# A second attention with three banks for each kind of scores, small reciprocals carried by DMA, and its copies moved one unit earlier

## What is computed

```python
h = N_HEAD                                      # 8
qk = jnp.einsum('bhdq,bhdl->bhql', qh, kh) * scale
sm = jax.nn.softmax(qk, axis=-1)
ret = jnp.einsum('bhql,bhdl->bhdq', sm, vh)     # 8 rows per head, 256 x 256 scores
return gamma * ret.reshape(B, Dv, Lq)
```

## Time and profile before

| what | value |
|---|---|
| time, median of 3 runs | 710.08 us (710.06 to 710.14) |
| the profiled execution's own time | 703.4 us |
| its span, first to last instruction | 701.7 us |
| mean granted clock | 0.946 of 2.4 GHz |
| PE busy over the span | 621.0 us (88%) |
| DVE, ACT, POOL busy | 497.5, 416.4, 309.3 us |
| second attention | about 258.6 to 508 us |
| of it, steps with both a tile `v` and a tile `t` | 15, about 14.0 us each |

### The profile page before, as it was taken

How to read it: one execution, slowest core, us unless ns; L and a number is a source line. 1 busy time by engine, 2 the same in 40 slices (tenths; PEclk the granted TensorE clock), 3 DMA queues, 4 the chain that set the end, 5 groups by cost and what they waited for, 6 DMA issues and landing times. The chain is left out here.

```text
span 701.7 us, 16803 instructions
## 1 busy us (share of the span) xinstructions
PE 621.0 (88%) x5077; PEld 463.5 (66%) x5077; DVE 497.5 (71%) x885; ACT 416.4 (59%) x829; POOL 309.3 (44%) x430
## 2 busy tenths in 40 slices
PE   3788878999999858999999999999679889999995
PEld 2677757788888745555545554555367779998884
DVE  3878784788887965788888888887437744444656
ACT  3888864434344513888888888888635235555430
POOL 2456554232323367365665565553144524124254
PEclk9999988999999965999999999999959979999999
DMA  5444459100000045244434443441001325446444
GB/s 159 114 112 120 134 148 306 43 1 1 0 0 15 10 114 148 82 134 115 114 104 134 113 114 104 133 112 31 1 2 45 121 90 186 146 148 178 126 132 125
DMA packets 70370, 70.42 MB, mean 100 GB/s; under 512 B 10421, under 2 KB 66581, under 8 KB 70325
## 3 DMA queue, kind: packets, MB, share of 16 engines
q1 hardware_dynamic: 65092, 55.55, 27.2%
q0 software_dynamic: 5232, 14.29, 6.9%
HBM read 38.22 MB, written 31.33 MB: 99 GB/s over the span
## 5 line engine op out<-in xcount | busy, mean ns | idle before, releaser
L1388 DVE TENSOR_REDUCE a_smax<-a_s 128x4 f32<-128x1024 f32 x128 | 154.3, 1214 | 35.1 <-PE a_s L1315 34.6
L1200 ACT ACTIVATE a_prob<-a_st 128x512 f32<-128x512 f32 x256 | 145.1, 593 | 29.4 <-PE a_st L1310 27.3
L1310 PEld LDWEIGHTS a_st<-qop,kop 25*128 25x128 f32 x512 | 66.0, 185 | 72.2 <-issue 51.5
L1315 PE MATMUL a_s<-kop,qop 24*128 24x256 f32 x512 | 104.3, 341 | 7.1 <-DVE a_smax L1388 4.8
L1310 PE MATMUL a_st<-qop,kop 25*128 25x256 f32 x512 | 105.4, 330 | 2.4 <-ACT a_prob L1200 1.9
L1255 PE MATMUL a_pv<-a_prob,a_vt 128*32 128x256 f32 x1024 | 81.6, 391 | 5.7 <-ACT a_pv_sb L1185 5.7
L816 POOL TENSOR_TENSOR f_hs_lo<-f_kept,f_hs_hi 128x512 fp32r<-128x512 f32 x32 | 41.3, 1324 | 87.7 <-ACT f_hs_hi L766 87.7
L1315 PEld LDWEIGHTS a_s<-kop,qop 24*128 24x128 f32 x512 | 65.1, 192 | 9.5 <-DVE a_smax L1388 6.1
L1833 POOL DMA_INDIRECT sorted_rows<-m_xn,m_slot x32 | 32.9, 1029 | 49.9 <-PE m_gu L126 27.2
L124 PE MATMUL f_bank<-f_xt_hi,w_hi 128*128 128x512 f32 x128 | 51.0, 398 | 1.2 <-DVE w_raw L859 0.6
L125 PE MATMUL f_bank<-f_xt_lo,w_hi 128*128 128x512 f32 x128 | 50.3, 393 | 0.0
(11 more groups left out here) (263 smaller groups left out, 1704.1 us busy)
## 6 DMA issues: line engine op xcount, KB each, us to landing
kop<-kop_rows SPq DMA_DIRECT2D x128, 48.0 KB
qop<-qop_rows SPq DMA_DIRECT2D x128, 48.0 KB
sorted_rows<-x_all SPq DMA_DIRECT2D x2, 2944.0 KB, 15.4
expert_rows<-turned SPq DMA_DIRECT2D x46, 128.0 KB
kop_rows<-k_hi SPq DMA_DIRECT2D x32, 128.0 KB, 2.3
qop_rows<-q_hi POOLq DMA_DIRECT2D x30, 128.0 KB, 2.6
qop<-sorted_rows SPq DMA_DIRECT2D x24, 128.0 KB, 2.2
kop<-sorted_rows SPq DMA_DIRECT2D x22, 128.0 KB, 2.4
```

Source lines behind the costliest of these rows:

```text
L1200: act.activation(prob[:, u % 8], st_ps[u % 2][:], ACT.Exp, scale=SCALE1).then_inc(prob_ready, 1)
L1310: st = pe.matmul(st_ps[u % 2][:, c * D:(c + 1) * D], lhsT=kop[t.slot][strip, u // 4, c * P:(c + 1) * P], rhs=qop[t.slot][strip, u // 4], s ...
L1315: sm = pe.matmul(s_ps[j % 2][:, k, c * D:(c + 1) * D], lhsT=qop[v.slot][strip, w // 4, c * P:(c + 1) * P], rhs=kop[v.slot][strip, w // 4], ...
L1388: dve.tensor_reduce(smax[:, v.slot, opposite(2 * j):opposite(2 * j) + 2].rearrange("p u q -> p (u q)"), s_ps[j % 2][:].rearrange("p u (q n ...
```

## The change

- **Banks.** `s_ps` and `st_ps` have three single banks each. `BANK[u]` is `u % 3`, and 1 for unit 15. Each unit waits for the last unit that used its bank (`after_last_use`). VectorE takes the maxima unit by unit, 16 instructions of 512 columns instead of 8 of 1024.
- **Order on TensorE.** Everything that is not scores stands behind an odd unit: `turn(t, 1)` and its `spare()` move from `u` = 2 to 1, both `selected` to 5, the context's transposes and their `spare()` from 14 to 13.
- **Order on ScalarE.** `weighted` moves from behind unit 3, 7, 11, 15 to behind unit 2, 6, 10, 14, and the copy to `a_back` from 9 to 8.
- **Reciprocals.** When the four quads of `o` are in SBUF, SP spreads the four rows of denominators (`den_rows`, 4 x 1024) over 128 partitions (`spread`, 128 x 32), VectorE takes one reciprocal of 128 x 32 at `u` = 9, and SP stores it back in place (`collect`). `selected` is done for tile `p = s - 4`, one step later than before, and waits for that store. GpSimd multiplies the two halves of `a_back`. `LAG` goes from 3 to 4.
- **Unread products.** `spare()` issues four matmuls instead of two in the steps whose `t` is tile 0 or 1.
- **End of the stage.** The transposes, copies and splits of `turned` stand at the start of step `DRAIN + 1` = 19 instead of behind the last step.

```diff
-        s_ps = [ctx.enter_context(nc.psum_tensor(f"a1_s{i}", [P, 2, 512], F32)) for i in range(2)]
-        st_ps = [ctx.enter_context(nc.psum_tensor(f"a1_st{i}", [P, 512], F32)) for i in range(2)]
+        s_ps = [ctx.enter_context(nc.psum_tensor(f"a1_s{i}", [P, 512], F32)) for i in range(3)]
+        st_ps = [ctx.enter_context(nc.psum_tensor(f"a1_st{i}", [P, 512], F32)) for i in range(3)]
...
-        rden = sb("a1_rden", [P, D], F32)
+        den = sb("a1_den", [P, UROWS], F32)
+        inverse = sb("a1_inverse", [P, UROWS], F32)
...
-        LAG = 3
+        LAG = 4
+        DRAIN = TILES + 2
...
+        BANK = [u % 3 for u in range(UNITS - 1)] + [1]
+        def after_last_use(eng, sem, step, u):
+            last = max(w for w in range(u - UNITS, u) if BANK[w] == BANK[u])
+            if last < 0:
+                after(eng, sem, step.plus(-1), UNITS, last + UNITS + 1)
+            else:
+                after(eng, sem, step, UNITS, last + 1)
...
+            def spread(o):
+                if o.inside(TILES):
+                    after(sp, pv_ready, o, QUADS)
+                    after(sp, inverse_ready, o.plus(-1))
+                    sp.dma_start(den[:], den_rows(o)).then_inc(den_spread[o.slot], 16)
...
+            def collect(o):
+                if o.inside(TILES):
+                    after(sp, inverse_ready, o)
+                    sp.dma_start(den_rows(o), inverse[:]).then_inc(inverse_stored[o.slot], 16)
...
             def step(s):
                 maxima(s.plus(-2), 1)
+                spread(s.plus(-3))
                 v = s.plus(-1)
                 if v.inside(TILES):
                     after(sp, vt_done, v.plus(-2))
                     sp.dma_start(ctx_t[:, v.slot], dram_at(d["ctx"], v.n)).then_inc(ctx_loaded[v.slot], 16)
                 load_operands(s, 0)
+                collect(s.plus(-3))
                 maxima(s.plus(-1), 0)
...
-                if o.inside(TILES):
-                    after(pool, rden_ready, o, 2)
-                    after(pool, x_ready, o.plus(-1))
-                    pool.tensor_tensor(att[:], back[:, 0], rden[:], ALU.mult).then_inc(att_ready, 1)
-                    after(pool, att_ready, o)
-                    pool.tensor_tensor(at(x_all, o.n), at(x_all, o.n), att[:], ALU.add).then_inc(x_ready, 1)
+                if p.inside(TILES):
+                    after(pool, back_ready, p)
+                    after(pool, x_ready, p.plus(-1))
+                    pool.tensor_tensor(att[:], back[:, 0], back[:, 1], ALU.mult).then_inc(att_ready, 1)
+                    after(pool, att_ready, p)
+                    pool.tensor_tensor(at(x_all, p.n), at(x_all, p.n), att[:], ALU.add).then_inc(x_ready, 1)
...
-                if s.known and s.n == TILES + LAG - 1:
+                if s.known and s.n == DRAIN:
                     norm.scalar(act, EARLY)
+                if s.known and s.n == DRAIN + 1:
+                    for dc in range(DC):
+                        turned.copy(act, FIRST, dc, s_ps[dc][:])
+                    turned.high(act, FIRST)
...
-                        act.activation(prob[:, u % 8], st_ps[u % 2][:], ACT.Exp, scale=SCALE1).then_inc(prob_ready, 1)
+                        act.activation(prob[:, u % 8], st_ps[BANK[u]][:], ACT.Exp, scale=SCALE1).then_inc(prob_ready, 1)
...
-                    if u == 3:
+                    if u == 2:
                         weighted(o, 3)
-                    if u == 9 and o.inside(TILES):
-                        after(act, sel_done, o)
-                        after(act, att_ready, o.plus(-1))
+                    if u == 8 and p.inside(TILES):
+                        after(act, sel_done, p)
+                        after(act, att_ready, p.plus(-1))
                         act.activation(back[:].rearrange("p m n -> p (m n)"), misc[:], ACT.Copy).then_inc(back_ready, 1)
...
-                    if u in (7, 11, 15):
-                        weighted(t, (u - 7) // 4)
+                    if u in (6, 10, 14):
+                        weighted(t, (u - 6) // 4)
...
-                        after(pe, pv_ready, w_, QUADS)
+                        after_dma(pe, inverse_stored, w_)
+                        after(pe, back_ready, w_.plus(-1))
...
+                        if t.known and t.n < 2:
+                            count *= 2
                         for g in range(count):
...
+                if s.known and s.n == DRAIN + 1:
+                    pe.wait_ge(turned.xn_ready, 1)
+                    pe.wait_ge(smax_ready, TILES * UNITS)
+                    for dc in range(DC):
+                        turned.transpose(pe, first_xn, dc, s_ps[dc][:], ident)
...
                             after_dma(pe, max_loaded[u // HALF], t)
-                        if u >= 2:
-                            after(pe, prob_ready, t, UNITS, u - 1)
-                        else:
-                            after(pe, prob_ready, t.plus(-1), UNITS, UNITS - 1 + u)
+                        after_last_use(pe, prob_ready, t, u)
...
-                        if k == 0 and j >= 2:
-                            after(pe, smax_ready, v, PAIRS, j - 1)
-                        elif k == 0:
-                            after(pe, smax_ready, v.plus(-1), PAIRS, PAIRS - 1 + j)
+                        after_last_use(pe, smax_ready, v, u)
...
-                    if v.inside(TILES) and k == 1:
+                    if v.inside(TILES):
                         sm.then_inc(s_done, 1)
-                    if u == 2:
+                    if u in (1, 3):
+                        products(o, 3, u // 2)
+                    if u == 1:
                         def before():
                             after(pe, vt_ready, t)
                             spare()
                         turn(t, 1, before)
-                    if u in (1, 3):
-                        products(o, 3, u // 2)
                     if u % 2 and u > 3:
                         products(t, u // 4 - 1, u % 4 // 2)
-                    if u in (6, 8):
-                        selected(o, u // 2 - 3)
+                    if u == 5:
+                        for m in range(2):
+                            selected(p, m)
                     if u == 11:
                         def before():
                             after(pe, neg_t_ready, t, 2)
-                            after(pe, back_ready, o)
+                            after(pe, back_ready, p)
                             spare()
                         turn(v, 0, before)
-                    if u == 14 and v.inside(TILES):
+                    if u == 13 and v.inside(TILES):
...
-                for j in range(PAIRS):
-                    if j == 4:
+                for u in range(UNITS):
+                    if u == 8:
                         negated(v, 0)
                     if v.inside(TILES):
-                        after(dve, s_done, v, PAIRS, j + 1)
-                        dve.tensor_reduce(smax[:, v.slot, opposite(2 * j):opposite(2 * j) + 2].rearrange("p u q -> p (u q)"),
-                                          s_ps[j % 2][:].rearrange("p u (q n) -> p (u q) n", q=2), AX_X, ALU.max).then_inc(smax_ready, 1)
-                    if j in (5, 6) and o.inside(TILES):
-                        cols = slice((j - 5) * P, (j - 4) * P)
-                        after(dve, back_ready, o)
-                        after(dve, att_ready, o.plus(-1))
-                        dve.reciprocal(rden[:, cols], back[:, 1, cols]).then_inc(rden_ready, 1)
-                    if j == 1 and s.known and s.n == TILES + LAG:
+                        after(dve, s_done, v, UNITS, u + 1)
+                        dve.tensor_reduce(smax[:, v.slot, opposite(u)], s_ps[BANK[u]][:].rearrange("p (q n) -> p q n", q=2),
+                                          AX_X, ALU.max).then_inc(smax_ready, 1)
+                    if u == 9 and o.inside(TILES):
+                        after_dma(dve, den_spread, o)
+                        after_dma(dve, inverse_stored, o.plus(-1))
+                        dve.reciprocal(inverse[:], den[:]).then_inc(inverse_ready, 1)
+                    if u == 2 and s.known and s.n == DRAIN + 1:
                         turned.low(dve, FIRST)
-                    if j == 1 and p.inside(TILES):
+                    if u == 3 and p.inside(TILES):
                         after(dve, x_ready, p)
                         dve.bn_stats(at(norm.stats, p.n), at(x_all, p.n)).then_inc(st_ready, 1)
```

32 lines of the change are left out of this document (13 added, 19 removed).

## The result

The changed kernel takes 721.96 us in the median (718.92 to 731.96), the kernel before beside it 710.07 us: a ratio of 1.0164, 95% interval [1.0129, 1.0200], or 12 us more. The forecast was 721.5. The sum came out, but not by its own terms: the steps at full clock did not grow, and the loss that was put down to them is TensorE's clock.

What follows compares the result with a forecast made beforehand. It took the chain of products block, ScalarE copy, `exp` and next block to set the step. Terms 4.9 + 0.2 + 2.0 + 0.7 + 1.1 + 0.3 + 2.2 = +11.4 gave 714.8 profiled, 721.5 with the median's 6.7 offset; range 708 to 730.

Steps and rivals of the forecast that it cites:

- the slower side: Whole kernel: all outcomes slower than the kernel before, given a chance of 0.78.
- The step, +4.9: Second attention, fourteen plain steps: each 14.3 us, 0.35 more than now, +4.9 us in all (-7 to +11).
- The list of segments: One step, P1 to P15 being products-block starts at odd units: eight predicted segments, 14.17 against 14.11 in the present step.
- Part 2: ScalarE: `weighted` ahead of `exp` of units 3, 7, 11, 15 delays it; block-to-block chain 1.65 against 1.00 of work.
- The clock, rival of 0.11: TensorE in the new step: idle some 2.9 us, its clock falls; five to ten falls add +8 to +17, 729 to 738.
- a granted clock under 1.00 between 300 and 480 us: TensorE in the second attention: listed among the signs that the forecast is wrong.
- Unread products, +2.0: Steps of tiles 0 and 1: two more matmuls in three places cost +2.0 us (1.4 to 2.4).
- The ends: Partial steps and last tile: +0.7 with only `v`, +1.1 with only `t`, 0.3 for last block's wait, +2.2 last tile.
- The step with only a tile `v`: Partial step, bound by VectorE: 16 x 0.61 less 8 x 1.13, +0.7 us.
- The step with only a tile `t`: Partial step, 12.11 us now: 13.2 by the segments, +1.1 us.
- The tail: Tile 15, last copy to addition: serial with two transfers, 7.9 us against 5.55, +2.3; taken as +2.2.
- copies do not bind: ScalarE copies, rival of 0.22: waits behind them shorter than read, joined pairs win a 13.4 us step, time 708.

Runs made afterwards that it cites:

- same_again: The changed kernel unaltered, run again for a second profile: 728.84 us in the median, ratio 1.0115 to the kernel before.
- copies_back: The changed kernel with only the weighted copies back behind exp of units 3, 7, 11 and 15: 718.49 us, ratio 1.0036 to the kernel before.
- before_again: The kernel before, unchanged, for a trace from the same chip as the others: 716.95 us, ratio 1.0026.
- fill_gaps: The changed kernel with two unread products in each of three TensorE waits per step: 717.06 us, ratio 1.0029 to the kernel before.
- late_values: The changed kernel with ScalarE reordered: maxima copy earlier, three weighted copies one unit later, copy to `a_vt` last: 704.97 us, ratio 0.9857 to the kernel before.
- late_tail: late_values with the last tile's denominators taken without transfers, by one reciprocal of 128x256 in place: 702.92 us, ratio 0.9904 to the kernel before.

## Why the prediction came out as it did

**Time and sign.** 721.5 was forecast, 721.96 came, and the slower side had 0.78. That the number fits so closely is chance: terms that were too large stand against one that was given a chance of 0.11 and no place in the sum. The 0.2% that a measurement was said to tell is too fine as well: six runs of the changed kernel lie between 718.92 and 731.96, and the interval is 0.36% to either side.

**The step, +4.9: wrong.** At full clock it is 14.03 (13.98 in same_again) against 14.00, so at most 0.4 us over fourteen. The list of segments was nearly right, 14.17 in sum against a measured 13.93. Five of eight lie within 0.07 of it (P1 to P3 1.66, P7 to P9 1.71, P9 to P11 1.13, P11 to P13 1.71, P13 to P15 1.86), and P3 to P5 is 1.80 for 1.65, since the copy of the maxima stood ahead of the weighted copy. Two were too long: P5 to P7 was put at 2.14 and is 1.88, since blocks of products that follow each other cost 0.45 and 0.43, and only the last one 0.55; P15 to P1 was put at 2.38 and is 2.18, since exp 14 starts 0.10 ahead of P15 and not behind it. Then 0.15 to 0.2 was added for gaps that the list did not know, because the same list gave 13.8 for the old order. That step failed: what the list lacked in the old order, the new one did not have. What held is Part 2: the three waits end with an `exp` behind a copy, and they eat up what the joined pairs save. copies_back limits that too: with the copies one unit later the blocks wait for the copy in place of the `exp`, and the step is 13.96.

**The clock, rival of 0.11: it is what happened.** Idle time was forecast as 2.9 of the step; it is 1.46, the sum of the three waits shown above. The price of a fall was put at 1.7 and is 2.4 us (16.43 to 16.45 for 14.03), more where it lasts longer (18.14). Four of fourteen steps fell in each of the two profiles of the changed kernel: 9.6 us of the 10.8 by which same_again's stage is longer than before_again's. Both profiles are of executions above their medians, 731.96 and 734.17 us; how many falls a run at the median has, no trace shows. The prediction listed "a granted clock under 1.00 between 300 and 480 us" among the signs that it is wrong, and that sign came. By the rival's own count of five to ten falls the time would have been 729 or more; it fell less often and the steps did not grow as well. In the Trainium skill, "TensorE: Matmul & The Clock Gate", section "A second HAM failure mode: psum-queue depth-cycling", short idles between groups of matmuls, with PSUM banks taken in turn, made the clock go up and down. The traces agree where TensorE is busy 90% with waits of 0.68, and fill_gaps shows the same step without the idles and the falls; copies_back, at the same 90% without a fall, is not told apart by that rule.

**Unread products, +2.0: too large.** 0.66 in the first two steps and 0.25 ahead of them. The prediction let waits cover only "a little" of them.

**The ends.** The step with only a tile `v` does not grow: from the stage's start to the first block 23.30 and 23.48 us against 23.23 and 23.81, for +0.7. The step with only a tile `t` takes 12.75 in same_again, +0.6 for +1.1; with a fall it took 16.50. The tail is 7.85 us for 7.9 in the first profile: that term, built from the price of a transfer of 128 KB, came out to 0.05, since one of 16 KB took the same 2.1. That close a fit is one profile's. In same_again the tail is 9.35, since the reciprocal stands behind normalisations that take 2.28 beside GpSimd, and `selected` runs at half clock; before_again has 6.49 for 5.55, so the difference is 2.3 in one pair of profiles and 2.9 in the other. The Trainium skill, "SBUF — State Buffer", section "The DMA setup-cost knee (why "@ 1 MiB" ≠ asymptote)", gives a transfer a fixed part of some 2 us that does not shrink with its bytes; 2.08 and 2.09 us, from the end of one engine's instruction to the start of the next one's, agree.

**What hid.** Reductions at 681 ns and 1.29 for two, the transfers covered in all steady steps, and the collected reciprocal never late: as forecast. The rival "copies do not bind" fell with the first look, and late_values put the price on it: taken off the chain, they are worth 0.8 us a step.

**The sum as measured**, from same_again against before_again: steps +9.2 (falls 9.6, the rest -0.4), the step with only `t` +0.6, the tail from the last copy to the last statistics +2.4 (10.17 for 7.75), less 1.4 at the ends (0.3 up to the first block, 0.6 from there to the first P15, 0.6 from the last P15 to the last copy): +10.8 in the stage. The forecast had +11.4.

## What to carry to other kernels

An engine that goes in order and waits for another puts everything behind it on the chain. So before banks or tiles are added, list for each copy which instruction of the same queue stands behind it and who waits for that one; here five copies on ScalarE in another order turned +12 us into -9, and without the change the one of these moves that was tried, the copy to `a_vt`, gave nothing. Unread products were free in a wait, where they held the clock, and lengthened the step without one: look at them again after every change of the order, in both directions. A longer lag costs slots: ask of each two-slot buffer who reads it last now.

## What had not been expected of the hardware

The clock of TensorE fell to 0.50 and came back inside a steady loop that repeats every 14.0 us, in different steps in two executions of the same kernel, at 90% busy (71.70 of 80 us). With the waits placed otherwise (71.83 of 80) it did not fall in any full step, nor in the kernels busy 74.35, 76.90, 77.70 and 78.93 of 80. No run tells what it is in the waits that counts.

Blocks of eight matmuls of 32 columns take 0.43 to 0.45 us when another such block follows (340.82, 341.27, 341.70), and 0.55 to 0.57 when scores follow (341.70 to 342.25, 349.11 to 349.68).

VectorE's SBUF work took longer where GpSimd ran beside it: the four normalisations take 1.38 us in the first profile of the changed kernel, with GpSimd idle, 2.28 in its second, with two GpSimd operations beside them, and 2.38 in late_tail, where its two operations lie beside them from 490.23 to 491.78. The split takes 2.00 in place of 1.29 there, and GpSimd's addition 1.05 in place of 0.72. The reductions, which read PSUM, keep their mean of 681 ns although GpSimd is busy 46.51 of 80 us.
